# Queries and keys of a cross-attention projected with channels on the partitions, rotated between two banks, and carried to the score stacks by DMA through a scratch array

## The chip, the cores and the metric

The kernel runs on one core of a Trainium2 chip. The metric is the device time of one execution in microseconds. A run of the kernel is one launch that computes four chained layers; the change touches the first two of the kernel's phases, which belong to the first layer.

## The reference, cut to what matters

Four batches of 512 tokens with 256 channels. The first layer is an attention of 16 heads of 16 channels from the normalised tokens to a context of the same size:

```python
t = _layernorm(x)                                  # (4, 512, 256)
q = (t @ Wq.T + bq).reshape(B, L, 16, 16).transpose(0, 2, 1, 3)
k = (ctx @ Wk.T + bk).reshape(B, K, 16, 16).transpose(0, 2, 1, 3)
v = (ctx @ Wv.T + bv).reshape(B, K, 16, 16).transpose(0, 2, 1, 3)
# rotation: x * cos + rotate_half(x) * sin, rotate_half = concat([-x2, x1]) of the two 8-channel halves
q, k = _apply_rope(q, cos_q, sin_q), _apply_rope(k, cos_k, sin_k)
attn = softmax(where(mask, q @ k^T * 16 ** -0.5, -inf))
x = x + tanh(g_xattn[0]) * mask * ((attn @ v) @ Wp.T + bp)
```

Three more layers follow (a mixture of experts, a second attention, a quantised feed-forward layer). The change doesn't touch them.

## The kernel before, in words

**The stacks.** `phase_attend` computes scores with matmuls whose two operands are "stacks": for every pair of heads, 128 partitions, 64 for each head (`ROWS`), and 512 tokens on the free axis. The 64 rows of a head are: three times 16 channels, so that high and low parts of the two operands give a product of near float32 precision (queries: high, high, low; keys: high, low, high), then four rows for the row maxima, one row for the mask, and rows of zeros. There are 32 pairs in all (8 for each batch), in `q_stacks` and `k_stacks`.

**phase_prepare** fills the stacks, tile by tile: 16 tiles (`T`) of 128 tokens with tokens on the partitions. For each tile TensorE transposes the normalised tokens (line 423), multiplies context by the key and value weights (430) and tokens by the query weights (436); VectorE adds the biases (292 to 297) and writes the values to `va`; GpSimd multiplies by cosine and sine (393 to 397); VectorE adds the two (303); ScalarE rounds the high parts into `stack` (347, 348); VectorE subtracts for the low parts (308, 310) and copies the mask (312); TensorE transposes `stack` 16 times, pair by pair (415), and ScalarE copies the result out of PSUM into `q_stacks` and `k_stacks` (355). `schedule` runs these as a software pipeline: engines work on tiles n+1, n, n-1, n-2 and n-3 in one step. Context arrives by tile through a pair of buffers, loaded from SP's queue (253).

**phase_attend** runs 16 steps (`STEPS`, four heads of one batch each). TensorE first computes scores only to find row maxima (500, 14 units of two heads ahead of use, `LEAD`), VectorE reduces them (562), GpSimd splits the maxima in two parts (`split`, 579 to 583), TensorE transposes these (510), ScalarE copies them (629), and GpSimd lowers the query stack by them (`lower`, 589). Then TensorE computes the scores again (518), ScalarE takes exponentials (638), and TensorE multiplies by the values (527). GpSimd also copies the values of a step to a padded tile (`stage_values`, 594) and adds a bias to one tile of x (`bias`, 600 and 604). Its order in step s is: `stage_values(s)`, `split(s + 1)`, `lower(s + 1)`, `bias(s)`. TensorE's order is written out in `block.tensor`; `values(s, 0)` waits for `v_ready`, `maxima(s + 1)` at key tile 2 waits for `mt_ready`.

Each phase is a block that all engines leave together before the next begins.

## Time and profile before

| | |
|---|---|
| Time before, median of 3 runs | 794.51 us (793.86 to 795.33) |
| Time of the profiled execution | 795.87 us |
| Its span, first to last instruction | 794.0 us |
| TensorE busy over the span | 689.2 us (87%) |
| VectorE busy | 473.1 us (60%) |
| ScalarE busy | 358.8 us (45%) |
| GpSimd busy | 283.2 us (36%) |
| Mean granted TensorE clock | 0.933 of full speed |

The shares of busy time are means over phases with different limits; what counts for this change is read from the stretch from 0 to about 180 us. A matmul in float32 appears as two records, so "x4" in a TensorE row are two products; in the scores of the attention a product is one record. In what follows PE is TensorE, DVE VectorE, ACT ScalarE, POOL GpSimd, SP SyncE, and a q behind the name is the engine's queue of DMA issues.

### The profile page before, as it was taken

What the parts mean: (1) busy time and instruction counts of PE and PEld (TensorE: products, weight loads), DVE (VectorE), ACT (ScalarE), POOL (GpSimd) and SP (SyncE); (2) the same over time, 40 slices, a digit from 0 to 9 for tenths busy, and PEclk for the clock granted to TensorE, in tenths of its full rate; (3) what the DMA queues carried; (4) which work ended last, traced back from release to release, by engine and by line L of the source; (5) the groups of instructions that cost most, each with busy time, mean ns of one, the idle gap of its engine ahead of it and who ended that gap; (6) DMA issues with size and microseconds to landing.
All of it is one profiled execution on the core that took longest, in us unless ns stands there. A gap on an engine that the chain in (4) does not pass through costs nothing. (4 is left out here: it accounts for less than half of the span.)

```text
span 794.0 us, 10607 instructions
## 1 busy us (share of the span) xinstructions
PE 689.2 (87%) x3503; PEld 441.0 (56%) x3522; DVE 473.1 (60%) x852; ACT 358.8 (45%) x644; POOL 283.2 (36%) x462
## 2 busy tenths in 40 slices
PE   3599959999999996878999999995699999966986
PEld 1277733433344333745777777774376776852554
DVE  3567658888888841746834343434355546447985
ACT  0156644888888886345432222431313031102665
POOL 1446523344433450580001010101040436246897
PEclk9799986999999999989999999998789899986999
DMA  6000000000000004800100000001100000000001
GB/s 195 14 27 26 20 8 0 1 1 1 1 1 1 1 1 164 314 15 0 70 37 1 1 0 0 1 0 43 25 1 0 1 1 0 1 0 2 26 33 47
DMA packets 14103, 21.43 MB, mean 27 GB/s; under 512 B 2161, under 2 KB 11505, under 8 KB 13297
## 3 DMA queue, kind: packets, MB, share of 16 engines
q1 hardware_dynamic: 13200, 20.34, 7.5%
q10 hardware_dynamic: 864, 0.59, 0.3%
q8 instruction: 23, 0.38, 0.2%
q14 instruction: 16, 0.12, 0.1%
HBM read 18.83 MB, written 2.10 MB: 26 GB/s over the span
## 5 line engine op out<-in xcount | busy, mean ns | idle before, releaser
L562 DVE TENSOR_REDUCE mx<-ps_f 128x2 f32<-128x1024 f32 x128 | 151.5, 1220 | 31.6 <-PE ps_f L500 31.3
L638 ACT ACTIVATE prob<-ps_s 128x512 f32<-128x512 f32 x256 | 134.6, 608 | 34.5 <-PE ps_s L518 34.5
L518 PE MATMUL ps_s<-q_stacks,k_stacks 64*128 64x512 f32 x256 | 90.2, 484 | 5.9 <-ACT prob L638 3.5
L518 PEld LDWEIGHTS ps_s<-q_stacks,k_stacks 64*128 64x128 f32 x256 | 35.8, 188 | 87.2 <-ACT prob L638 70.9
L500 PE MATMUL ps_f<-k_stacks,q_stacks 64*128 64x512 f32 x256 | 63.8, 449 | 6.8 <-DVE mx L562 5.3
L527 PE MATMUL ps_o<-prob,vst 128*32 128x512 f32 x512 | 69.0, 612 | 0.0
L1018 ACT ACTIVATE qs<-ps_g 128x512 f32<-128x512 f32 x40 | 23.9, 598 | 88.6 <-PE ps_u L902 88.6
L1085 DVE SCALAR_TENSOR_TENSOR h<-ps_u,most,qs 128x512 f32<-128x512 f32 x32 | 24.0, 751 | 62.5 <-ACT qs L1018 62.5
L589 POOL TENSOR_TENSOR q_stacks<-minus,q_stacks 128x1024 fp32r<-128x1024 f32 x16 | 38.0, 2372 | 55.0 <-ACT minus L629 55.0
L172 POOL TENSOR_TENSOR norm_tmp_att<-st 128x4 f32<-128x4 f32 x4 | 1.0, 240 | 142.4 <-DVE st L1124 142.4
L1527 ACT ACTIVATE qs<-ps_SC,nmax 128x512 f32<-128x512 f32 x16 | 11.0, 686 | 76.4 <-DVE nmax L1415 76.4
L1091 DVE TENSOR_TENSOR h_low<-h,h_high 128x512 fp32r<-128x512 f32 x40 | 27.6, 691 | 23.4 <-ACT h_high L1022 23.2
L1022 ACT CAST h_high<-h 128x512 fp32r<-128x512 f32 x40 | 24.8, 621 | 31.2 <-DVE h L1085 31.2
L500 PEld LDWEIGHTS ps_f<-k_stacks,q_stacks 64*128 64x128 f32 x256 | 30.8, 197 | 14.2 <-DVE mx L562 11.7
L393 POOL TENSOR_TENSOR qkr<-qkb,c 128x512 f32<-128x512 f32 x16 | 20.3, 1268 | 42.5 <-DVE stack L312 30.1
L1299 PE MATMUL ps_SC<-ks 128*128 128x512 f32 x64 | 31.8, 644 | 3.3 <-DVE ks L1409 2.3
L347 ACT CAST stack<-qkr 128x512 fp32r<-128x512 f32 x16 | 9.9, 618 | 54.0 <-DVE qkr L303 30.8
L430 PE MATMUL ps_kv<-wkv,ctxT 128*128 128x512 f32 x64 | 34.3, 663 | 0.0
L415 PE MATMUL ps_st<-c,stack 128*128 128x128 f32 x256 | 30.8, 274 | 3.9 <-ACT q_stacks L355 3.9
L1317 PE MATMUL ps_q<-ks,qs 128*128 128x256 f32 x128 | 30.9, 384 | 1.5 <-DVE hq L1444 1.5
L415 PEld LDWEIGHTS ps_st<-c,stack 128*128 128x128 f32 x256 | 28.7, 142 | 6.3 <-DVE stack L312 2.3
L916 PE MATMUL ps_yE<-h_high,down_low 128*128 128x512 f32 x80 | 32.1, 402 | 0.0
(278 smaller groups left out, 1524.2 us busy)
## 6 DMA issues: line engine op xcount, KB each, us to landing
up<-in_up SPq DMA_DIRECT2D x10, 256.0 KB, 6.7
x<-in_x SPq DMA_DIRECT2D x4, 512.0 KB, 8.0
ctxT<-in_ctxT SPq DMA_DIRECT2D x16, 128.0 KB, 2.1
ks<-in_ctxTC SPq DMA_DIRECT2D x1, 2048.0 KB, 13.3
ks<-in_ctx SPq DMA_DIRECT2D x1, 2048.0 KB, 18.8
out<-x SPq DMA_DIRECT2D x16, 128.0 KB, 1.7
down<-in_down SPq DMA_DIRECT2D x1, 1280.0 KB, 5.5
ks<-in_wqv SPq DMA_DIRECT2D x1, 1024.0 KB, 20.7
```

What stands on the lines that cost most here:

```text
L415: last = pe.transpose(ps_st[i][:, p, :], stack[:, u, i // 2, 2 * pair:2 * pair + 2, :] .rearrange("p h r -> p (h r)"), id32)
L430: last = pe.matmul(ps_kv[u][:, :, :], ctxT[:, u, c, :], wkv[:, c, :, :], start=(c == 0), stop=(c == DC - 1))
L500: last = pe.matmul(ps_f[n % 2][:, h, :], qs[rows(h), 2 * f + pair, qt * P:(qt + 1) * P], ks[rows(h), 2 * f + pair, :], start=True, stop=True)
L518: pe.matmul(ps_s[n % 3][:, :], ks[rows(h), 2 * s + pair, kt * P:(kt + 1) * P], qs[rows(h), 2 * s + pair, :], start=True, stop=True).then_i ...
L527: last = pe.matmul(ps_o[HPAD * j:HPAD * (j + 1), :], vst[:, s % 2, kt, HPAD * j:HPAD * (j + 1)], prob[:, kt % 2, j, :], start=(kt == 0), s ...
L562: dve.tensor_reduce(mx[:, f % 2, qt, 2 * pair:2 * pair + 2], ps_f[n % 2][:, :, :], AX_X, ALU.max).then_inc(used, 1)
L589: pool.tensor_tensor(own, minus[:, :, :].broadcast_to([P, 2, S]), own.bitcast(F32), ALU.add)\
L638: act.activation(prob[:, kt % 2, j, :], ps_s[n % 3][:, :], ACT.Exp, scale=SCALE)\
L916: pe.matmul(ps_y[half][:, :], down_low[:, e, own], h_high[:, u, :], start=False, stop=False)
L1091: dve.tensor_tensor(h_low[:, u, :], h32[:, u, :], h_high[:, u, :].bitcast(F32), ALU.subtract)\
L1299: last = pe.matmul(ps_S[q % 2][:, :], sT[:, c, q * P:(q + 1) * P], ctxT[:, c, ds(b * S, S)], start=(c == 0), stop=(c == DC - 1))
L1317: last = pe.matmul(ps_q[:, :], attT[:, q % 2, k, :], ctok[:, ds(b * QT + k, 1), :], start=(k == 0), stop=(k == QT - 1))
```

## The change

**What it does.** Queries and keys are computed with channels on the partitions and a whole batch (512 tokens) on the free axis, in two banks of 128 channels (the columns of the weights are sorted on the host so that bank 0 holds the first halves of all heads, bank 1 the second halves). The rotation then is: bank times cosine, bank times sine, and a difference and a sum between the banks (`turn_parts` on VectorE, `add_parts` on GpSimd). High parts are rounded on ScalarE, low parts subtracted on VectorE for keys (`low_k`) and GpSimd for queries (`low_q`), in place over `part`. The 16 stack transposes per tile and the copies behind them are gone. Instead SP writes high and low parts, 512 KB each, to a scratch array in HBM (`Stacks.write`), and GpSimd reads them back into the rows of the stacks (`Stacks.read`: six DMAs for a batch's queries or keys, 16 partitions and 256 KB each). The fixed rows and the mask row also come by GpSimd's DMAs. Reads of batches 0 and 1 (keys) lie in `phase_prepare`, those of batch 1 (queries), 2 and 3 in `phase_attend`, in GpSimd's order ahead of `stage_values`. Normalising moves from VectorE to ScalarE. Context comes by batch, and the loads of batches 2 and 3 lie in SP's queue behind writes.

```diff
-C_ID, C_COS, C_SIN, C_TRI, C32 = 0, 128, 192, 256, 320
+C_ID, C_TRI, C32 = 0, 128, 192
...
+        turned["spent"] = [parts, summed, high_done, k_low, q_low, q_done, v_done, v_copied, k_done, xT_done]
         @block.sync
...
+            def load_ctx(b):
+                if b > 1:
+                    sp.wait_ge(k_done, b - 1)
+                    sp.wait_ge(v_done, QT * (b - 1))
+                sp.dma_start(ctx_raw[:, b % 2, :, :], a["ctxTC"][:, :, b * S:(b + 1) * S]).then_inc(ctx_in[b % 2], 16)
             load_x(0)
+            sp.dma_start(wk, a["wk"]).then_inc(wk_in, 16)
+            load_ctx(0)
+            sp.dma_start(trig[:, :, :], a["trig"]).then_inc(wk_in, 16)
+            sp.dma_start(wv[:, :, :], a["wv"]).then_inc(weights, 16)
+            sp.dma_start(wq[:, :, :], a["wq"]).then_inc(weights, 16)
+            load_x(1)
+            load_ctx(1)
+            for b in range(2, B):
                 load_x(b)
+            for b in range(B):
+                sp.wait_ge(high_done, 2 * b + 1)
+                stacks.write(sp, "k", b, 0, k_out)
+                sp.wait_ge(k_low, b + 1)
+                stacks.write(sp, "k", b, 1, k_out)
+                if b + 2 < B:
+                    load_ctx(b + 2)
+                sp.wait_ge(high_done, 2 * b + 2)
+                stacks.write(sp, "q", b, 0, turned["q_out"])
+                sp.wait_ge(q_low, b + 1)
+                stacks.write(sp, "q", b, 1, turned["q_out"])
+            sp.wait_ge(k_out, 32 * B)
+        @block.tensor
+        def _(pe):
+            def keys(b):
+                pe.wait_ge(ctx_in[b % 2], 16 * (b // 2 + 1))
+                wait(pe, parts, 2 * b - 1)
+                for c in range(DC):
+                    for d in range(DC):
+                        last = pe.matmul(ps_k[c][:, :], wk[:, d, c * P:(c + 1) * P], ctx_raw[:, b % 2, d, :],
+                                         start=(d == 0), stop=(d == DC - 1))
+                last.then_inc(k_done, 1)
+            def queries(b):
+                pe.wait_ge(xT_copied, b + 1)
+                wait(pe, parts, 2 * b)
+                for c in range(DC):
+                    for d in range(DC):
+                        last = pe.matmul(ps_q[c][:, :], wq[:, d, c * P:(c + 1) * P], xnT[:, d, :], start=(d == 0),
+                                         stop=(d == DC - 1))
+                last.then_inc(q_done, 1)
+            def values(b):
+                for q in range(QT):
+                    if q % 2 == 0:
+                        wait(pe, v_copied, QT * (b - 1) + q + 2)
+                    for d in range(DC):
+                        last = pe.matmul(ps_v[q // 2][:, q % 2, :], ctx_raw[:, b % 2, d, q * P:(q + 1) * P], wv[:, d, :],
+                                         start=(d == 0), stop=(d == DC - 1))
+                    last.then_inc(v_done, 1)
+            def transposes(b):
+                wait(pe, xT_copied, b)
+                for q in range(QT):
+                    pe.wait_ge(xn_ready, QT * b + q + 1)
+                    for c in range(DC):
+                        last = pe.transpose(ps_T[:, c, q * P:(q + 1) * P], xn[:, q, c * P:(c + 1) * P], id32)
+                last.then_inc(xT_done, 1)
+            pe.wait_ge(wk_in, 32)
+            keys(0)
...
+            for b in range(B):
+                if b:
+                    keys(b)
+                transposes(b)
+                values(b)
+                queries(b)
         @block.vector
         def _(dve):
+            def turn_parts(b, which):
+                done, held, out = ((k_done, ps_k, k_out), (q_done, ps_q, turned["q_out"]))[which]
+                n = 2 * b + which
+                dve.wait_ge(done, b + 1)
+                wait(dve, out, 32 * b)
+                wait(dve, summed, n)
+                for c in range(DC):
+                    dve.scalar_tensor_tensor(out=part[which][:, c, :], in0=held[c][:, :], scalar=bqk[:, which, c:c + 1],
+                                             in1=trig[:, 0, :], op0=ALU.add, op1=ALU.mult)
+                for c in range(DC):
+                    last = dve.scalar_tensor_tensor(out=turn[:, 1 - c, :], in0=held[c][:, :],
+                                                    scalar=bqk[:, which, c:c + 1], in1=trig[:, 1, :], op0=ALU.add,
+                                                    op1=ALU.mult)
+                last.then_inc(parts, 1)
+            def low_k(b):
+                dve.wait_ge(high_done, 2 * b + 1)
+                dve.tensor_tensor(low[OF_K][:, :, :], part[OF_K][:, :, :], high[OF_K][:, :, :].bitcast(F32), ALU.subtract)\
+                   .then_inc(k_low, 1)
...
+            for b in range(B):
...
+                turn_parts(b, OF_K)
...
+                    ln_vector(dve, b + 1, (QT * (b + 1), QT * (b + 2)))
+                copy_values(b)
+                low_k(b)
+                turn_parts(b, OF_Q)
         @block.scalar
         def _(act):
+            def normalise(b):
+                act.wait_ge(rstd_ready, b + 2)
+                wait(act, xT_done, b)
+                for q in range(QT):
+                    t = QT * b + q
+                    act.activation(xn[:, q, :], x_sb[:, t, :], ACT.Identity, bias=less_mean[:, t:t + 1])\
+                       .then_inc(centred, 1)
+                for q in range(QT):
+                    t = QT * b + q
+                    act.wait_ge(centred, t + 1)
+                    act.activation(xn[:, q, :], xn[:, q, :], ACT.Copy, scale=rstd[:, t:t + 1]).then_inc(xn_ready, 1)
+            def transposed(b):
+                act.wait_ge(xT_done, b + 1)
+                wait(act, q_done, b)
+                act.copy(xnT[:, :, :], ps_T[:, :, :]).then_inc(xT_copied, 1)
+            def high_part(b, which):
+                act.wait_ge(summed, 2 * b + which + 1)
+                act.copy(high[which][:, :, :], part[which][:, :, :]).then_inc(high_done, 1)
...
+            for b in range(B):
+                transposed(b)
+                high_part(b, OF_K)
+                if b + 1 < B:
+                    normalise(b + 1)
+                high_part(b, OF_Q)
         @block.gpsimd
         def _(pool):
+            def add_parts(b, which):
+                pool.wait_ge(parts, 2 * b + which + 1)
+                pool.tensor_tensor(part[which][:, 0, :], part[which][:, 0, :], turn[:, 0, :], ALU.subtract)
+                pool.tensor_tensor(part[which][:, 1, :], part[which][:, 1, :], turn[:, 1, :], ALU.add).then_inc(summed, 1)
+            def low_q(b):
+                pool.wait_ge(high_done, 2 * b + 2)
+                pool.tensor_tensor(low[OF_Q][:, :, :], part[OF_Q][:, :, :], high[OF_Q][:, :, :].bitcast(F32), ALU.subtract)\
+                    .then_inc(q_low, 1)
             ln_pool(pool, 0, (0, QT))
+            stacks.fixed_rows(pool, "q", 0, B - 1)
+            stacks.fixed_rows(pool, "k", 0, B - 1)
+            pool.wait_ge(mask_done, 2)
+            for b in range(B - 1):
+                stacks.mask_row(pool, b)
+            for b in range(B):
+                add_parts(b, OF_K)
+                if b:
+                    low_q(b - 1)
+                if b == 1:
+                    pool.wait_ge(k_out, 32)
+                    stacks.read(pool, "k", 0)
+                if b == 2:
+                    pool.wait_ge(turned["q_out"], 32)
+                    stacks.read(pool, "q", 0)
+                if b == 3:
+                    pool.wait_ge(k_out, 32 * 2)
+                    stacks.read(pool, "k", 1)
+                if b + 1 < B:
+                    ln_pool(pool, b + 1, (QT * (b + 1), QT * (b + 2)))
+                add_parts(b, OF_Q)
+            low_q(B - 1)
+class Stacks:
...
+    def fixed_rows(self, pool, name, b, batches):
+        for h in range(2):
+            at = ROWS * h + MAX_ROW
+            n = ROWS - MAX_ROW - (name == "k")
+            dst = self.to[name][at:at + n, 8 * b:8 * (b + batches), :].rearrange("r (s a) n -> r s (a n)", a=2)
+            pool.dma_start(dst, self.a[name + "rows"].broadcast_to([n, 4 * batches, 2 * S])).then_inc(self.landed[b], 16)
+    def mask_row(self, pool, b):
+        for h in range(2):
...
+            pool.dma_start(self.to["k"][at:at + 1, 8 * b:8 * b + 8, :], src).then_inc(self.landed[b], 16)
+    def write(self, sp, name, b, part, out):
+        src = self.turned["low" if part else "high"][name == "q"]
+        sp.dma_start(self.a["room_" + name][b, part], src[:, :, :].bitcast(F32)).then_inc(out, 16)
+    def read(self, pool, name, b):
+        for o, part in enumerate((0, 0, 1) if name == "q" else (0, 1, 0)):
+            src = self.a["room_" + name][b, part].rearrange("(s a i) c n -> a (i c) s n", a=2, s=H // 2)
+            for h in range(2):
+                at = ROWS * h + HD * o
+                pool.dma_start(self.to[name][at:at + HD, 8 * b:8 * b + 8, :], src[h]).then_inc(self.landed[b], 16)
 def phase_attend(...)
...
+                if n % (UNITS * NG) == 0:
+                    pe.wait_ge(turned["landed"][f // NG], 16 * (14 + 4 * (f in (0, STEPS - NG))))
...
+            def stacks_ahead(s):
+                if s == 0:
+                    pool.wait_ge(turned["q_out"], 32 * B)
+                if s == 1:
+                    stacks.read(pool, "k", 2)
+                if s == 2:
+                    stacks.read(pool, "q", 2)
+                if s == 4:
+                    stacks.fixed_rows(pool, "k", 3, 1)
+                    stacks.mask_row(pool, 3)
+                    stacks.read(pool, "k", 3)
+                if s == 5:
+                    stacks.fixed_rows(pool, "q", 3, 1)
+                    stacks.read(pool, "q", 3)
+            pool.wait_ge(turned["q_out"], 32 * 2)
+            stacks.read(pool, "q", 1)
...
             for s in range(STEPS):
+                stacks_ahead(s)
                 if s > 1:
                     stage_values(s, s % 2)
```

All lines of the former tile pipeline in `phase_prepare` are removed. `part` and `low` are one piece of memory, for keys and for queries.

## Rows read from the trace of the kernel before

**Rows 1.** Busy time by stretch: start and end, length, each engine's us (instructions), clock, DMA
```profile
30.00:40.00 10.00, 3.78 (x6) 1.83 (x7) 5.01 (x19) 1.14 (x2) 4.58 (x4) 0.58 0.04 14
60.00:70.00 10.00, 10.00 (x62) 7.79 (x61) 7.39 (x22) 6.67 (x14) 6.19 (x8) 1.00 0.09 26
...
120.00:130.00 10.00, 8.38 (x30) 4.36 (x28) 9.14 (x9) 4.00 (x8) 3.18 (x6) 0.50 0.00 0
...
150.00:160.00 10.00, 9.82 (x64) 4.12 (x66) 8.35 (x8) 8.34 (x17) 3.73 (x6) 1.00 0.00 0
```

**Rows 2.** Timeline at the seam of the two phases: start, duration, instruction
```profile
108.06 1.18 ACT L355 CAST k_stacks<-ps_st 128x512 fp32r<-128x512 f32 x2
109.49 0.34 SPq L490 DMA_DIRECT2D bp<-in_bp  x1
```

**Rows 3.** Timeline of PE in the preparation, 36 to 50 us
```profile
36.70 3.62 PE L430 MATMUL ps_kv<-wkv,ctxT 128*128 128x512 f32 x4
...
43.76 1.88 PE L430 MATMUL ps_kv<-wkv,ctxT 128*128 128x512 f32 x4
45.48 1.03 PE L436 MATMUL ps_qA<-wq,xnT 128*128 128x256 f32 x4
...
48.09 0.38 PE L423 MATMUL ps_T<-c,xn 128*128 128x128 f32 x2
48.31 1.88 PE L430 MATMUL ps_kv<-wkv,ctxT 128*128 128x512 f32 x4
```

**Rows 4.** Throughput of the DMA engines, 40 slices of 4 us from 0 to 160 us
```profile
GB/s 43 342 358 192 33 0 33 33 2 0 33 12 25 33 33 33 33 33 33 26 7 33 33 2 0 0 4 34 1 0 0 0 0 0 0 0 4 0 0 0
```

**Rows 5.** Groups of DVE and ACT instructions: count, busy us, mean ns, idle time before
```profile
L1085 DVE SCALAR_TENSOR_TENSOR h<-ps_u,most,qs 128x512 f32<-128x512 f32 x32 | 24.0, 751 | 62.5 <-ACT qs L1018 62.5
L1107 DVE TENSOR_TENSOR x_low<-qs,x_high 128x1024 fp32r<-128x1024 f32 x4 | 5.1, 1274 | 2.4 <-ACT x_high L1006 2.3
...
L1006 ACT CAST x_high<-qs 128x1024 fp32r<-128x1024 f32 x4 | 4.2, 1052 | 0.0
```

**Rows 6.** Groups of POOL instructions
```profile
L589 POOL TENSOR_TENSOR q_stacks<-minus,q_stacks 128x1024 fp32r<-128x1024 f32 x16 | 38.0, 2372 | 55.0 <-ACT minus L629 55.0
L393 POOL TENSOR_TENSOR qkr<-qkb,c 128x512 f32<-128x512 f32 x16 | 20.3, 1268 | 42.5 <-DVE stack L312 30.1 <-DVE qkb L297 12.4
...
L148 POOL TENSOR_TENSOR rstdA<-lntmpA,powerA 128x4 f32<-128x4 f32 x1 | 1.0, 1034 | 6.9 <-DVE lntmpA L139 6.9
```

**Rows 7.** DMA issues over the whole run: count, KB each, median us from issue to landing
```profile
x<-in_x SPq DMA_DIRECT2D x4, 512.0 KB, 8.0
...
out<-x SPq DMA_DIRECT2D x16, 128.0 KB, 1.7
```

**Rows 8.** Timeline of the issues of two DMAs over 128 partitions, on SP's and ACT's queue
```profile
1.25 0.66 SPq L249 DMA_DIRECT2D wkv<-in_wk  x1
...
3.33 1.03 ACTq L368 DMA_DIRECT2D bv<-in_bv  x1
```

**Rows 9.** Timeline of POOL: first split, one step, start of the next
```profile
119.43 0.29 POOL L579 TENSOR_SCALAR mt<-mx 128x16 fp32r<-128x16 f32 x1 [7.07 <-DVE mx L562]
...
159.66 0.61 POOL L600 TENSOR_TENSOR gated<-bp,coef 128x256 f32<-128x256 f32 x1
...
161.03 0.42 POOL L594 COPY vst<-va 128x272 f32<-128x272 f32 x1
164.15 0.27 POOL L579 TENSOR_SCALAR mt<-mx 128x16 fp32r<-128x16 f32 x1 [2.70 <-DVE mx L562]
...
164.82 0.27 POOL L583 TENSOR_SCALAR mt<-mt 128x16 f32<-128x16 f32 x1
...
170.88 0.60 POOL L600 TENSOR_TENSOR gated<-bp,coef 128x256 f32<-128x256 f32 x1
```

**Rows 10.** Timeline of PE in the same step
```profile
165.29 1.07 PE L527 MATMUL ps_o<-prob,vst 128*32 128x512 f32 x8
...
166.96 0.66 PE L510 MATMUL ps_s<-c,mt 128*128 128x128 f32 x4
```

304 lines of the change are left out of this document (97 added, 207 removed).

## The prediction

> **What bounds the kernel now.** I read the profile from the outside in. The table of stretches shows where the change lies: once it runs, PE is busy for all 10 us of a stretch of the preparation at full clock, with DVE at 7.4 and POOL at 6.2 [rows 1]; before that there is a slow start, with PE at 3.8 of 10 us and a clock of 0.58. The timeline at the seam says when the preparation ends: the last copy out of PSUM ends at 109.2 us and the attention's first DMA is issued at 109.5 [rows 2]. The timeline of PE gives the pitch: from one key and value product to the next it is 48.31 - 43.76 = 4.55 us for a tile [rows 3], so PE's work per tile, the 16 stack transposes among it, sets the pace. In the attention PE is busy for 9.8 of 10 us, DVE and ACT for 8.3 [rows 1]: whatever stalls PE there lengthens the kernel by the same amount, and POOL, with 3.7 us of 10, has room. Its step lasts 170.88 - 159.66 = 11.2 us [rows 9].
>
> **PE's share of the preparation.** Two float32 products with 512 columns take 1.88 us at full clock, 3.62 at the low one; two with 256 columns take 1.03, two transposes 0.38 [rows 3]. A batch now costs PE 4 products of 512 for keys and 4 for queries (3.8 us each), 8 of 256 for values (some 3.8) and 8 transposes (1.5): 12.9 us, against 4 x 4.55 = 18.2 before. So PE would need 52 us for four batches and no longer sets the pace, unless its clock stays low.
>
> **The start.** Before keys(0) the loads of x (512 KB), wk (256), context (512), trig (512) and about 100 KB of constants must land. The DMA engines moved 0.17, 1.37 and 1.43 MB in the first three slices of 4 us [rows 4]. 1.9 MB are through at 9.1 us, and with a us for the receipt keys(0) starts at 10.2. The first products run at the low clock, as the product at 36.70 us did [rows 3]: 4 x 1.81 = 7.2, to 17.4. Transposes, values and queries at full clock take 9.1 more, to 26.5. turn_parts is four DVE instructions of 0.75 us [rows 5], which overlap a little: 2.8. add_parts is two POOL instructions of half the size of the 2.37 us one: 2.4 [rows 6]. So the queries' sum of batch 0 ends at 31.7. The keys' side of batch 0 is earlier: turn_parts ends at 20.2, when POOL has issued its ten DMAs for fixed rows and masks (10 + 10 x 0.8 = 18, price below).
>
> **The loop from batch to batch.** Three loops are closed in the new code, and the longest one sets the pitch.
> The first runs through HBM: `low_q` lies in the memory of `part`, so turn_parts of the queries waits until the low part of the batch before is written (`q_out`), and POOL makes that low part only behind the keys' sum. In order: turn_parts K 2.8, add_parts 2.4, low_q 2.4 [rows 5, 6], the write W, turn_parts Q 2.8, add_parts 2.4, which is 12.8 + W. For W the nearest rows are a store of 128 KB with 1.7 us to landing and loads of 512 KB, issued among others, with 8.0 [rows 7]; these are the bounds. The write has 512 KB and lands beside POOL's six reads of 256 KB, so I take 5.0, between the two. Pitch: 17.8.
> The second runs through POOL: add_parts Q 2.4, wait for turn_parts K 2.8, add_parts K 2.4, low_q 2.4, six DMA issues at d each, the power 1.0 [rows 6]: 11.0 + 6d. It becomes the longest at d = 1.13.
> The third spans two batches: power, normalising on ACT (eight instructions of some 0.4, my estimate from 1.05 us for four times the elements [rows 5]: 3.2), values and queries 7.6, then turn and add of queries and keys 10.4, low_q 2.4, 6d, 1.0, some 25 + 6d for two batches, 15 for one at d = 0.8. ScalarE has some 7 us of work in a batch and DVE 12; neither binds.
> So three pitches of 17.8 from 31.7 lead to 85.1. Behind it stand the last high part 1.05 [rows 5], low_q 2.4 and an issue with the change of blocks 0.9: 89.4. PE now has 12.9 us of work in 17.8, with pauses of some us in front of the transposes, and the clock was at 0.58 with PE at 3.8 of 10 us in the old preparation and at 0.50 in the attention's first steps with PE at 8.4 of 10 [rows 1]. One batch's values and queries at the low clock would cost 7.6 more, all of them hidden where that loop has slack; I add 3. Preparation ends at 92.5 and gives 109.2 - 92.5 = 16.7 us.
>
> A page of the Trainium skill, "DMA: Bandwidth & Descriptors" (Anatomy of one DMA), gives about 2.0 us and bytes over 436 GB/s for a DMA, which is 3.2 us for such a write. By it the sum would be 3 x 1.8 = 5.4 us lower. The store of 128 KB above took 1.7, less than the page's 2.3, and the loads in a crowd took far more than its formula, so I stay with the rows.
>
> **What is given back in the attention.** POOL issues its DMAs ahead of `stage_values(s)`: 6 at s = 1 and 2, 10 at s = 4, 8 at s = 5. Behind them on POOL are the copy of the values, which PE needs for values(s, 0), and split(s + 1), which PE needs for the transposed maxima. The rows give the slack: the copy ended at 161.45 and the product that uses it began at 165.29: 3.84 us. The split waited 2.70 us for DVE, and was done at 165.09 where PE came to it at 166.96 [rows 9, 10]: 4.6, and 5.0 at s = 1, where there is no copy. Past the slack, PE stands still, and DVE and ACT behind it.
> The price d of one issue on POOL is not in the trace, since POOL issued no DMA. Bounds: 0.34 us, the shortest issue on SP [rows 2], and 1.9, if POOL stands to the 1.03 us of the dearest issue over 128 partitions [rows 8] as its elementwise work stands to DVE's (2.37 against 1.27 for 1,024 elements [rows 5, 6]). A read has 128 runs of 2 KB, as many as the two issues of [rows 8] have partitions; I take 0.8 between these. Then 6 issues cost 4.8: nothing at s = 1, 1.0 at s = 2; 8.0 - 3.84 = 4.2 at s = 4; 6.4 - 3.84 = 2.6 at s = 5. Sum 7.8. The six issues at the head of the attention are free: POOL waited 7.07 us for DVE before its first split [rows 9]. If that cover were gone they would cost 4.8.
> The waits of PE on the landing of a batch cost nothing in the forecast: batch 0's reads are issued by 63 us, batch 1's by 97 and needed in step 2, some 35 us on; later ones have longer.
> The same page says that a DMA from GpSimd is prepared in software with about 1 us to the first byte, against 0.6 us from SP or ACT. No row here shows it. With d = 1.0 the sum of the stalls would be 1.0 + 2.2 + 6.2 + 4.2 = 13.6.
>
> **Sum.** -16.7 + 7.8 = -8.9. Against the profiled execution, 795.87 - 8.9 = 787.0; that one lay 1.4 us over the median of 794.51, so I predict 786.
>
> **Rivals.**
> 1. *POOL's issues are dear, and the kernel gets slower.* The mechanism is the one place of PE's wait for the copied values and the split. At d = 1.1 stalls of 1.6 + 2.8 + 7.2 + 5.0 = 16.6 use up the gain: above 1.1 the kernel is slower. At d = 1.4 stalls are 3.4 + 4.6 + 10.2 + 7.4 = 25.6, POOL's loop is 19.4, which puts the seam at 97.3, and the sum is +13.7: 808. For it speaks that POOL is the slowest engine in each shared kind of work, against it the 0.66 us of an issue on SP [rows 8].
> 2. *POOL's issues are cheap and the write is quick.* d = 0.6 and W = 3: stalls 0 + 0 + 2.2 + 1.0 = 3.2, seam at 86.5, sum -19.5: 775. With d = 0.34, W = 1.7 and no cold batch the seam is at 79.6 and nothing is given back: 765.
> 3. *PE's clock stays low through the preparation.* Then 10.2 + 4 x 25.4 us and the tail of 9 give 121, and with the stalls +20: 814. For it speaks the clock of 0.50 to 0.58 with PE partly idle [rows 1], against it that keys, transposes and values run back to back for some 9 us in every batch.
> 4. *POOL's transfers are slow.* Fixed rows of 3.1 MB and batch 0's reads of 3.1 MB go through POOL's queue from 11 us on; below 6.3 MB / 81 us = 77 GB/s the first product of the attention waits. Each has a destination of 16 partitions; if rate followed partitions, an eighth of the 358 GB/s of [rows 4] would be 45 GB/s, the landing at 151, and the time near 844. The Trainium skill's "SBUF — State Buffer" (The DMA port swizzle) has it that the number of ports reached decides, and 16 neighbouring partitions reach 4 of 16; by that the rate would be some 109 GB/s and nothing would wait. No row here shows either.
> 5. *Gain and loss cancel*, d near 1.1, within 0.2%.
>
> **How the numbers follow.** Forecast (d 0.7 to 1.0, W 3.5 to 6.5) 0.36, its own range 778 to 793; rival 2 0.27; rival 5 0.07; rival 1 0.17; rival 4 0.07; rival 3 0.06. About 0.2% is what a measurement of this kernel tells from no change. Faster 0.36 + 0.27 = 0.63, same 0.07, slower 0.30. The range goes from 766, the low bounds of d and W, to 808, rival 1 at 1.4: outside are rival 4, most of rival 3 and the dear end of rival 1.
>
> **What the profile will show.** If I am right: the seam near 92; PE at 7 of 10 us in the preparation; DVE's turn_parts of the queries released by a DMA of q_out, or POOL's by d, with a pitch of 17 to 18; rows of POOL's queue near 0.8 us each; idle time of PE of 1, 4 and 3 us in steps 2, 4 and 5 and none in 1; from step 6 on the pitch of 11.2 as before, and nothing changed behind the attention. The prediction is wrong if POOL's issues cost over 1.1 us, if the write loop isn't the longest, if PE's first product waits for a landing, or if the clock in the preparation is at 0.5 throughout.

## The result, and the profile after

| | before | after |
|---|---|---|
| Median | 794.35 us (4 runs, 793.86 to 795.33) | 814.89 us (4 runs, 813.3 to 815.5) |
| Profiled execution, span | 795.87, 794.0 us | 815.22, 812.7 us |
| Seam | 109.5 us | 124.1 us |
| Seam to the end | 684.5 us | 688.6 us |

The ratio is 1.026 (95% interval 1.024 to 1.027): slower by 20 us, where 786 was forecast. The seam is the point at which the attention's first DMA is issued; "seam to the end" is the span less that point.

The busy times by stretch, against [rows 1]: between 40 and 50 us no compute engine does anything, yet the DMA engines move 225 GB/s.

```profile
30.00:40.00 10.00, 5.37 (x16) 2.57 (x14) 0.00 (x0) 1.96 (x2) 0.30 (x1) 0.92 1.31 136
40.00:50.00 10.00, 0.00 (x0) 0.00 (x0) 0.00 (x0) 0.00 (x0) 0.00 (x0) 0.50 1.03 225
60.00:70.00 10.00, 5.82 (x20) 5.05 (x21) 3.60 (x5) 5.26 (x10) 4.39 (x5) 0.66 1.42 187
...
126.00:138.00 12.00, 8.62 (x24) 3.52 (x24) 11.13 (x11) 0.59 (x1) 5.70 (x13) 0.50 1.40 120
```

DVE's timeline says what ends that silence. These are the first rows of turn_parts of the keys of batches 1, 2 and 3 and of the last low part; the bracket holds the idle time and who ended it:

```profile
50.09 1.41 DVE L328 SCALAR_TENSOR_TENSOR k_part<-ps_k,bqk,trig 128x512 f32<-128x512 f32 x2 [22.36 <-DMA room_k<-k_low_part]
...
59.66 1.21 DVE L338 TENSOR_TENSOR k_low_part<-k_part,k_high 128x1024 fp32r<-128x1024 f32 x1
...
74.34 1.41 DVE L328 SCALAR_TENSOR_TENSOR k_part<-ps_k,bqk,trig 128x512 f32<-128x512 f32 x2 [10.28 <-DMA room_k<-k_low_part]
...
98.21 1.41 DVE L328 SCALAR_TENSOR_TENSOR k_part<-ps_k,bqk,trig 128x512 f32<-128x512 f32 x2 [9.92 <-DMA room_k<-k_low_part]
```

The pitch is 23.9 to 24.3 us, and the sum by group (count, busy us, mean ns, idle time before) puts nearly all the waits on the keys' write, hardly any on the queries'. The last row is the price d of an issue on POOL:

```profile
L328 DVE SCALAR_TENSOR_TENSOR k_part<-ps_k,bqk,trig 128x512 f32<-128x512 f32 x8 | 5.6, 747 | 50.0 <-DMA room_k<-k_low_part 42.6 <-PE ps_k L278 7.5
L328 DVE SCALAR_TENSOR_TENSOR q_part<-ps_qA,bqk,trig 128x512 f32<-128x512 f32 x8 | 5.6, 745 | 3.4 <-DMA room_q<-q_low_part 2.5 <-issue 0.9
...
L477 POOL DMA_DIRECT2D k_stacks<-room_k x12 | 6.4, 537 | 0.0
```

The DMA issues up to 125 us (count, KB each, median us from issue to landing), against [rows 7], and below them the issues of 24 to 52 us, where the low part of batch 0's keys takes 24.9 us:

```profile
k_stacks<-room_k POOLq DMA_DIRECT2D x12, 256.0 KB, 11.0
...
room_k<-k_low_part SPq DMA_DIRECT2D x4, 512.0 KB, 13.2
...
room_q<-q_low_part SPq DMA_DIRECT2D x4, 512.0 KB, 3.5
q_stacks<-in_qrows POOLq DMA_DIRECT2D x2, 768.0 KB, 18.1
...
k_stacks<-in_krows POOLq DMA_DIRECT2D x2, 720.0 KB, 31.0
...
room_k<-k_low_part SPq DMA_DIRECT2D x1, 512.0 KB, 24.9
```

At the seam, against [rows 2], POOL has been idle for 5.92 us:

```profile
124.10 0.33 SPq L518 DMA_DIRECT2D bp<-in_bp  x1
124.11 0.95 POOL L599 MEMSET mt<- 128x1024 f32 x1 [5.92 <-POOLq L202]
```

The keys' last write is not what it waits for. POOL's reads of batch 1's keys, issued from 105.75 us on, landed up to 122.66, while that write had landed at 117.93. In the twelve runs in which DMAs of POOL's were still in flight when its last instruction ended, the seam followed 0.9 to 1.7 us behind the last landing; in e4, which has none, it followed POOL's last instruction by 0.8. So the blocks seem to change only when POOL's own DMAs have landed; no run tests that apart.

In the attention, against [rows 9], these are the starts of steps 4, 5 and 6 and what POOL issues in step 4:

```profile
185.46 0.61 POOL L632 TENSOR_TENSOR gated<-bp,coef 128x256 f32<-128x256 f32 x1
186.82 1.23 POOL L460 DMA_DIRECT2D k_stacks<-in_krows  x2
188.03 1.07 POOL L466 DMA_DIRECT2D k_stacks<-mrow  x2
189.10 3.15 POOL L477 DMA_DIRECT2D k_stacks<-room_k  x6
...
198.35 0.61 POOL L632 TENSOR_TENSOR gated<-bp,coef 128x256 f32<-128x256 f32 x1
...
210.03 0.61 POOL L632 TENSOR_TENSOR gated<-bp,coef 128x256 f32<-128x256 f32 x1
```

Step 4 lasts 12.89 instead of 11.2 us, step 5 11.68: stalls of 1.7 and 0.5.

### The profile page after: what moved, and what is told of

Read it like the earlier page. It is cut to its first block and busy times, and to the rows that moved or that the text cites. A ratio compares the mean times of both kernels' runs of the same rounds, so it can differ in the third digit from the quotient of the medians.

```text
span 812.7 us, 9603 instructions
## 1 busy us (share of the span) xinstructions
PE 665.6 (82%) x3266; PEld 415.4 (51%) x3266; DVE 462.2 (57%) x775; ACT 334.9 (41%) x592; POOL 304.2 (37%) x496
## 5 line engine op out<-in xcount | busy, mean ns | idle before, releaser
L1068 ACT ACTIVATE qs<-ps_g 128x512 f32<-128x512 f32 x40 | 23.9, 599 | 89.3 <-PE ps_u L952 89.2
L278 PE MATMUL ps_k<-ctx_raw,wk 128*128 128x512 f32 x32 | 19.4, 764 | 30.2 <-DVE turn L331 19.6
L1141 DVE TENSOR_TENSOR h_low<-h,h_high 128x512 fp32r<-128x512 f32 x40 | 27.6, 691 | 23.4 <-ACT h_high L1072 23.2
L328 DVE SCALAR_TENSOR_TENSOR k_part<-ps_k,bqk,trig 128x512 f32<-128x512 f32 x8 | 5.6, 747 | 50.0 <-DMA room_k<-k_low_part 42.6
L1611 POOL TENSOR_TENSOR ehT<-ks,hqT 128x256 f32<-128x256 f32 x16 | 11.8, 741 | 55.5 <-DVE hqT L1498 40.9
L278 PEld LDWEIGHTS ps_k<-ctx_raw,wk 128*128 128x128 f32 x32 | 7.7, 251 | 40.8 <-issue 26.7
L1758 ACT ACTIVATE qs<-ps_gD,amax 128x1024 f32<-128x1024 f32 x16 | 17.8, 1115 | 25.5 <-PE ps_gD L1796 25.5
## 6 DMA issues: line engine op xcount, KB each, us to landing
k_stacks<-room_k POOLq DMA_DIRECT2D x24, 256.0 KB, 10.3
ctx_raw<-in_ctxTC SPq DMA_DIRECT2D x4, 512.0 KB, 16.7
```

Of the source, the lines that this page charges most:

```text
L278: last = pe.matmul(ps_k[c][:, :], wk[:, d, c * P:(c + 1) * P], ctx_raw[:, b % 2, d, :], start=(d == 0), stop=(d == DC - 1))
L1141: dve.tensor_tensor(h_low[:, u, :], h32[:, u, :], h_high[:, u, :].bitcast(F32), ALU.subtract)\
```

## The experiments

Theory 1: the DMAs with destinations of 16 partitions on POOL's queue hold up SP's writes, and DVE waits for the write of the keys' low part because `low` lies in the memory of `part`. The rival, theory 2: a write of 512 KB to HBM is slow by itself. Letters behind a theory's number are local to the run that they stand with. In e1, e3 and e4 a block of zeros ahead moves the first load from 0.74 to 18.20 us, so 17.5 us are to be taken off every point of time and off the total.

**e3_no_fixed: no fixed rows of batches 0 to 2.**

```diff
-            stacks.fixed_rows(pool, "q", 0, B - 1)
-            stacks.fixed_rows(pool, "k", 0, B - 1)
```

> Leaves out the four DMAs of fixed rows of batches 0 to 2 (3 MB), with both stacks set to zero in a block of some 17 us ahead of everything, so times count from the first load. Theory 1 (the writes to the scratch array stand behind GpSimd's transfers on the shared DMA engines): the wait of 22.4 us in front of the keys' turn_parts of batch 1 falls to under 6, the later two waits of 10 us stay, and the seam of the phases comes some 17 us earlier, near 107 us from the start of the loads. Theory 2 (a write of 512 KB to HBM is slow by itself, 10 us or more): the first wait falls to about 10 at most and the seam by under 13.

813.25 us, or 795.8 without the zeros; seam 124.4 - 17.5 = 106.9. The wait of 22.4 us is gone, the two of 10 us are there. Without the 3 MB of constants the first wait doesn't come about.

**e4_no_early: no DMA of POOL's for batches 0 to 2.**

```diff
-            stacks.fixed_rows(...)       # "q" and "k", batches 0 to 2, and their mask rows
-                    stacks.read(...)     # all reads of batches 0 to 2
```

> Leaves out every GpSimd DMA of batches 0 to 2 (fixed rows, masks, reads), with the same block of zeros ahead; the scores of these batches are zero. The writes to the scratch array stay. Theory 1: each write of 512 KB lands within 3 to 4 us, no turn_parts waits over 2 us for it, the pitch of a batch is near 15 us and the seam near 85 us from the start of the loads (39 earlier than in the changed kernel). Theory 2: writes still land after 10 us, the pitch stays near 24.

789.01 us, or 771.5 without the zeros; seam 100.2 - 17.5 = 82.7. SP's writes are unchanged, but land in 2.6 to 3.5 us (medians; 3 to 4 were expected), and turn_parts of the keys is released by POOL's sum, at a pitch of 16.1:

```profile
64.17 1.41 DVE L328 SCALAR_TENSOR_TENSOR k_part<-ps_k,bqk,trig 128x512 f32<-128x512 f32 x2 [2.70 <-POOL q_part L419]
80.28 1.41 DVE L328 SCALAR_TENSOR_TENSOR k_part<-ps_k,bqk,trig 128x512 f32<-128x512 f32 x2 [2.70 <-POOL q_part L419]
```

```profile
room_k<-k_low_part SPq DMA_DIRECT2D x4, 512.0 KB, 2.9
room_q<-q_high SPq DMA_DIRECT2D x4, 512.0 KB, 2.6
```

**e1_spread: batch 0 to 2's reads to 128 partitions, same bytes.**

```diff
-                pool.dma_start(self.to[name][at:at + HD, 8 * b:8 * b + 8, :], src[h])...
+                pool.dma_start(self.to[name][:, at, :], self.a["zeros"][:, h, :])...   # at = 8 * b + 2 * o + h
```

> The six reads of each set (batches 0 to 2) have the same bytes, run length and number of runs, but each goes to one slot of all 128 partitions in place of eight slots of 16 partitions; they read an array of zeros in HBM. Fixed rows stay narrow. Block of zeros ahead. Theory 1a (the narrow destination makes GpSimd's transfers slow): a set of 1.6 MB lands in 5 us in place of 13, the waits of 10 us in front of batches 2 and 3 fall under 5, that of batch 1 (22 us) stays, the seam comes some 12 us earlier. Theory 1b (the software queue or the rounding on the way makes them slow): the rate stays near 120 GB/s and the waits as they were.

820.43 us; seam 129.3 - 17.5 = 111.8, 12.3 us earlier than with narrow reads. The first wait stays at 22.45, the others fall to 5.9 and 6.4 us, where under 5 was expected.

**e5_probe: narrow and wide transfers by themselves**, ahead of the changed kernel.

```diff
+ for o in range(3): for h in range(2):
+   eng.dma_start(to[64 * h + 16 * o:64 * h + 16 * o + 16, :, :], rows16[h])   # narrow
+   eng.dma_start(to[:, 2 * o + h, :], rows128[h])                             # wide
```

> A block ahead of the changed kernel moves seven sets of six DMAs of 256 KB from HBM, one set after the other, each awaited: GpSimd to 16 partitions with rounding, GpSimd to 16 without, GpSimd to 128 partitions with rounding, to 128 without, SP to 16, SP to 128, and SP with ACT to 16 each at once. Theory 1a: sets to 16 partitions take some 13 us whatever the queue, sets to 128 some 5. Theory 1b: GpSimd's sets take 13 us whatever the width, SP's 5; if rounding is the cost, only the sets with it.

The last column is GB/s. In order: POOL narrow with rounding, POOL narrow, POOL wide with rounding, POOL wide, SP narrow, SP wide, SP and ACT narrow at once, each into its own half:

```profile
2.00:14.00 12.00, 0.00 (x0) 0.00 (x0) 0.00 (x0) 0.00 (x0) 2.74 (x6) 1.00 1.43 130
18.00:29.00 11.00, 0.00 (x0) 0.00 (x0) 0.00 (x0) 0.00 (x0) 1.36 (x3) 1.00 1.03 133
31.00:37.00 6.00, 0.00 (x0) 0.00 (x0) 0.00 (x0) 0.00 (x0) 3.14 (x6) 1.00 0.81 229
39.00:44.00 5.00, 0.00 (x0) 0.00 (x0) 0.00 (x0) 0.00 (x0) 2.73 (x6) 1.00 0.76 250
47.00:58.00 11.00, 0.00 (x0) 0.00 (x0) 0.00 (x0) 0.00 (x0) 0.00 (x0) 1.00 1.00 139
60.00:66.00 6.00, 0.00 (x0) 0.00 (x0) 0.00 (x0) 0.00 (x0) 0.00 (x0) 1.00 0.82 260
68.00:79.00 11.00, 0.00 (x0) 0.00 (x0) 0.00 (x0) 0.00 (x0) 0.00 (x0) 1.00 1.02 141
```

Neither the queue nor the rounding matters much; the destination does. From first issue to last landing a narrow set took 13.3 to 14.6 us, a wide one 7.1 to 7.9, not the 5 expected. Two queues, each into its own half of the partitions, move no more together than one queue that alternates between the halves.

**e9_width: how wide is wide enough, and what it does to a write.** The same six DMAs of 256 KB from SP on 16, 32, 64 and 128 neighbouring partitions and on 16 that lie eight apart; then a write beside a crowd on ACT's queue.

> Edit: a block of transfers ahead of the changed kernel, some 75 us of it, the rest as it is. From SP's queue five sets of six DMAs, 256 KB each in 128 runs of 2 KB: 16 neighbouring partitions, 32, 64, 128, and 16 partitions eight apart. Then from ACT's queue six of the narrow ones, with one write of 512 KB from SP's queue behind the first of them; the same with six of the wide ones; and the write alone. Theory A (the rate follows the ports of the SBUF that the partitions reach: 4, 8, 8, 16 and 8 of 16): 13, 7, 7, 5 and 7 us. Theory B (the rate follows the number of partitions, whichever they are): 13, 7, 4 to 5, 4 to 5 and 13 us. For the write both have: over 8 us behind narrow reads, 4 to 6 behind wide ones, 3 alone; the rival, that a write is only slow by its share of the bytes, has the same time in both crowds.

Rates in that order (last column); the sixth row is the narrow crowd with the write in it, and below stands the landing of the write in the narrow crowd, in the wide crowd and alone:

```profile
5.00:14.00 9.00, 0.00 (x0) 0.00 (x0) 0.00 (x0) 0.00 (x0) 0.00 (x0) 1.00 1.08 121
20.00:26.00 6.00, 0.00 (x0) 0.00 (x0) 0.00 (x0) 0.00 (x0) 0.00 (x0) 1.00 1.03 214
29.00:35.00 6.00, 0.00 (x0) 0.00 (x0) 0.00 (x0) 0.00 (x0) 0.00 (x0) 1.00 1.02 230
38.00:41.00 3.00, 0.00 (x0) 0.00 (x0) 0.00 (x0) 0.00 (x0) 0.00 (x0) 1.00 0.98 308
44.00:50.00 6.00, 0.00 (x0) 0.00 (x0) 0.00 (x0) 0.00 (x0) 0.00 (x0) 1.00 0.98 215
56.00:65.00 9.00, 0.00 (x0) 0.00 (x0) 0.00 (x0) 0.00 (x0) 0.00 (x0) 1.00 1.08 120
...
room_q<-q_high SPq DMA_DIRECT2D x1, 512.0 KB, 11.5
...
room_q<-q_high SPq DMA_DIRECT2D x1, 512.0 KB, 6.5
...
room_q<-q_high SPq DMA_DIRECT2D x1, 512.0 KB, 2.6
```

For these transfers theory A's order holds: 64 partitions are hardly better than 32 (230 against 214), and 16 partitions spread out are as good as 32 neighbours (215); the five times were 15.6, 9.4, 9.1, 6.8 and 9.7 us, a fifth to two fifths above those expected. By the port formula of the Trainium skill's "SBUF — State Buffer" (Door 1: The DMA port swizzle) these reach 8 of 16 ports, 16 neighbours reach 4. Its asymptotes are 109 and 218 GB/s; measured are 121 (130 to 141 in e5) and 214 to 230, so the ratio agrees and the narrow rate lies above the page's. The same page says that two DMAs into the two halves at once serialize; e5's last row, 141 GB/s, agrees.

The write in the narrow crowd was issued at 57.55 us and landed at 69.09. It didn't share the engines: from 58 to 65.5 us ACT's queue moved 490 packets and SP's none, and from 65.5 to 69.2 SP's 144 and ACT's last 59.

**e13_small_packets and e14_half_reads: how the queues share the engines.** e13 sends each fixed-row DMA as two, with runs of 2 KB instead of 4; e14 sends three of the six reads of batch 0's keys later.

```diff
-            pool.dma_start(dst, self.a[name + "rows"].broadcast_to([n, 4 * batches, 2 * S]))...
+            for a in range(2):
+                dst = self.to[name][at:at + n, 8 * b + a:8 * (b + batches):2, :]
+                pool.dma_start(dst, self.a[name + "rows"][:, :, a * S:(a + 1) * S].broadcast_to(...))...
```
```diff
-                    stacks.read(pool, "k", 0)
+                    stacks.read(pool, "k", 0, (0,))                       # b == 1
...
-                    stacks.read(pool, "k", 1)
+                    stacks.read(pool, "k", 0, (1,)); stacks.read(pool, "k", 1, (0,))   # b == 3; the rest at the head of the attention
```

> Edit: the changed kernel with the fixed rows of a half sent in two DMAs of 2 KB packets instead of one of 4 KB packets; the same rows, partitions and bytes. Nothing is left out. Theory 1a (the two queues take turns packet by packet, and the narrow packets set the pace of both): against 4 KB packets a queue of 2 KB packets gets a third of some 125 GB/s, against 2 KB packets half of it; the write of the keys' low part of batch 0 lands after 14 to 19 us instead of 25, the first wait in front of turn_parts of the keys shrinks from 22.4 to 11 to 17 us, the other two stay at 10; four more issues on GpSimd at the start and two in steps 4 and 5 cost 1 to 3 us; time 806 to 812 us. Theory 1b (the write waits until all narrow bytes that were sent before it are through): the bytes are the same, the wait stays at 21 to 24 us and the time at 815 to 818 us.

> Edit: the changed kernel with only three of the six reads of batch 0's keys (one half of the stacks) where all six stood; the other three go where batch 1's keys were read, three of whose six go to the head of the attention. Nothing is left out. Theory 1a (turns packet by packet): the 512 packets of SP's queue (keys' high and low part of batch 1) now have turns with 384 narrow packets instead of 512 of 768; the second wait shrinks from 10.3 to 6 to 9 us, and that the doubled reads added nothing there is the other end of the same curve; the first wait (22 us) and the third (10) stay. Time 809 to 814 us. Theory 1b (all narrow bytes sent before it): 3 reads are 6 us less, the second wait is 4 to 5 us. Rival (the wait doesn't depend on the reads): it stays at 10 us.

The second row of turn_parts of the keys in e13, and the third in e14:

```profile
42.33 1.41 DVE L328 SCALAR_TENSOR_TENSOR k_part<-ps_k,bqk,trig 128x512 f32<-128x512 f32 x2 [15.21 <-DMA room_k<-k_low_part]
```

```profile
69.37 1.41 DVE L328 SCALAR_TENSOR_TENSOR k_part<-ps_k,bqk,trig 128x512 f32<-128x512 f32 x2 [5.72 <-DMA room_k<-k_low_part]
```

With the same bytes in smaller runs the first wait fell from 22.4 to 15.2 us (the write landed after 17.7 instead of 24.9; 809.05 us in all), though the last fixed rows landed no sooner, at 46.4 us instead of 44.7. That is the queues taking turns, not a write behind all bytes sent before it. The packet counts of the two queues show the turns directly. From 16 to 32 us of the changed kernel POOL's queue moved 441 packets with 1.62 MB and SP's 441 with 0.45 MB; in e13 it was 830 and 765. SP's packets have 1 KB on average, and they are not the write's: they are the rows of x of batches 2 and 3 (1 MB), which SP had issued before it. The second of these loads, issued at 7.11 us, landed at 48.17; the keys' low part, behind it in the same queue, at 50.01. So 1 MB in small packets ahead of the first write took turns with POOL's packets of 4 KB. At this stretch's 27.6 packets per us the 256 packets of the keys' high and low part, issued from 22.9 us on, would have taken 9 us by themselves: an estimate of 32 to 35 us for the landing instead of 50. No run moved these loads, so that is not tested.

In e14 the second wait fell from 10.3 to 5.7, below the 6 to 9 of the turns and above the 4 to 5 of the other theory: the wait depends on the reads, but the run doesn't choose between the two. (Its count of packets was off as well: a write goes in 128 packets of 4 KB, so high and low part are those 256, not 512.) The third wait stayed at 10.1; 808.92 us.

**e11_twice and e10_wide_reads.** e11 sends batch 0's key reads twice; e10 writes the high part twice to the scratch array so that a read is one DMA over 48 partitions.

```diff
+                    stacks.read(pool, "k", 0, 1)      # e11: again, into batch 1's rows
...
+        all_three = self.a["room_" + name][b].rearrange("(s a i) u c n -> a (i u c) s n", a=2, s=H // 2)   # e10
+            to = self.to[name][ROWS * h:ROWS * h + MAX_ROW, 8 * b:8 * b + 8, :]
+            pool.dma_start(to, all_three[h])...
```

> Edit: the changed kernel with the suspected cost doubled in one place. The six reads of batch 0's keys are sent a second time right behind the first, into the rows of batch 1, which get their own later. Theory 1: the write of the low part of the keys of batch 1 now stands behind 3.1 MB at some 125 GB/s instead of 1.6; the wait in front of turn_parts of the keys of batch 2 grows from 10 us by 10 to 13, the first wait (22 us) stays, and the time grows by as much, to 824 to 829 us. Rival (the write waits for something else, its own length or the engines' order): the waits stay as they are, the time grows by 0 to 3 us, which the six more issues on GpSimd may cost.

> Edit: the changed kernel with wide reads. The high part is written twice to the scratch array, beside the low part, so that the 48 rows of a half of the stacks are one DMA over 48 neighbouring partitions, 768 KB (rows in another order, the same for queries and keys, which leaves the sums of products the same). Two reads for a batch's queries or keys instead of six, the same bytes; the write of the high part has 1 MB instead of 0.5. Fixed rows as they are. Theory 1 (the width of the destination sets the rate, and the reads hold up the write of the keys' low part): a batch's reads take 7 to 8 us instead of 13, the second and third wait in front of turn_parts of the keys shrink from 10 to 3 to 6 us each, the first of 22 us, which is the fixed rows', stays; with two issues instead of six on GpSimd the stalls in steps 4 and 5 are gone. Seam at 109 to 116, time 796 to 805 us. Rival (bytes or the number of transfers in flight count, not the width): the waits stay at 10 us or grow with the larger write, time 812 us or more.

Both expectations failed. In e11 (814.42 us) the second wait stayed at 9.93. Seen afterwards, the write had landed at 73.1 us and the sixth of POOL's reads landed only at 76.4, so the six added behind them came too late to matter. The extra reads delayed something else, turn_parts of the queries of batch 2 (7.5 us idle), and the third key wait shrank to 2.7, so nothing was added. In e10 (807.34 us) the waits are 23.2, 8.8 and 8.2. A high part of 1 MB now stands ahead of the low part in SP's queue, so the run weighs two changes against each other and doesn't isolate the width. Nor were its reads quick: over 48 partitions they moved 132 GB/s from 124 to 136 us, where almost nothing else went, against 120 for the narrow ones, and the queries of batch 1 took 14.1 us instead of 15.2, not 7 to 8. That doesn't fit theory A, which gives 48 neighbours the rate of 32. Why they are slow here, and not in e9, is open.

**e6_late_fixed and e7_two_k: the two remedies apart.** e6 sends batch 1's and 2's fixed rows at the head of the attention; e7 keeps the order and gives the keys' high and low parts two copies.

```diff
-            stacks.fixed_rows(pool, "q", 0, B - 1)
+            stacks.fixed_rows(pool, "q", 0, 1)            # e6; "k" likewise
...
-                wait(dve, out, 32 * b)
+                wait(dve, out[b % 2], 32 * (b // 2))      # e7, keys only; part, high, low indexed by b % 2
```

> Edit: ahead of the preparation only batch 0's fixed rows are sent (1 MB); those of batches 1 and 2 (2 MB) go behind the reads at the head of the attention. Nothing is left out of the computation. Theory 1 (the fixed rows, 16 partitions wide, hold the DMA engines when the low part of the keys of batch 0 is to be written): 1 MB at about 130 GB/s is through at 20 us, the write is issued at 25 us and lands in under 8 us; the wait of 22.4 us in front of turn_parts of the keys of batch 1 goes, the two waits of 10 us behind it stay, the seam comes at 107 to 108 and the time is 796 to 800 us. Rival (the write is late because of the crowd of loads at the start, or the reads that follow): that wait stays above 10 us and the time above 804 us.

> Edit: two copies of the keys' high part and low part, used in turn (the second lies in the rows of batch 3, which are filled much later); DMAs and their order are as in the changed kernel. Nothing is left out. Theory 1 (slow writes, and someone who waits for them): the writes of the keys' low parts land as late as now, 25 and 13 us, but VectorE's turn_parts of the keys no longer waits for them; the wait moves to GpSimd in front of batch 0's reads (k_out) and to turn_parts of the queries (q_out). So part of the 42.6 us of waits comes back as others: seam 106 to 118, time 795 to 809 us. Rival (the memory shared by parts is the whole cause, the slow transfers are not): the pitch falls to 15 to 16 us at once, seam 84 to 88, time 773 to 778 us. Second rival (the wait is only a symptom of another chain): seam 122 to 126.

e6: 797.94 us, seam 105.8 (107 to 108 expected); the first wait gone, the others 10.3 and 9.9. e7: 793.0 us, 2 us below the range, seam 102.7 (106 to 118). As expected POOL now waits for the write, though only once. What was not expected: DVE waits for the same queue all the same, 16 us, for x of batches 2 and 3. Afterwards turn_parts of the keys goes at 16.7:

```profile
48.52 1.41 DVE L121 BATCH_NORM_STATS2 st<-x 128x6 f32<-128x256 f32 x4 [16.04 <-DMA x<-in_x]
...
50.70 3.19 POOL L482 DMA_DIRECT2D k_stacks<-room_k  x6 [13.36 <-DMA room_k<-k_low_part]
```

**e8_all and e12_all_wide: both remedies, and transfers spread over the steps.** Two copies for queries too; fixed rows batch by batch; no more than six issues in one step of the attention.

```diff
-                    pool.wait_ge(k_out, 32 * 2)
-                    stacks.read(pool, "k", 1)
+                    stacks.fixed_rows(pool, "q", 1, 1)
+                    stacks.fixed_rows(pool, "k", 1, 1)
...
+                if s in (1, 4):    # fixed rows of batches 2 and 3, and 3's mask row
+                if s in (2, 5):    # k reads;  s in (3, 6): q reads;  batch 1's: k at the head, q in step 0
```

> Edit: the candidate for a faster kernel. Two copies of high and low parts of keys and of queries; ahead of the preparation only batch 0's fixed rows, batch 1's where the keys of batch 1 were read; the reads of batch 1's keys at the head of the attention, its queries in step 0, then one group of at most six reads in each of steps 2, 3, 5 and 6, fixed rows in 1 and 4. Nothing is left out. Theory 1: no wait on a write is left, the pitch is set by GpSimd or by the chain through both engines, 14 to 16 us; batch 0's reads (24 us at 130 GB/s) end before the seam at 82 to 88; no stall in steps 4 and 5; time 766 to 776 us. Rival (the transfers cost as much wherever they stand, and the first product of batch 1 or batch 0 waits for its rows instead): time above 785 us.

> Edit: the faster candidate (two copies, spread transfers) with the wide reads. Theory 1: in the candidate no wait on a transfer was left, and the pitch of 16.1 us is VectorE's own work and one addition on GpSimd, which wide reads don't touch; only the tail and the first steps of the attention can gain. Seam at 83 to 86, time 768 to 772 us, the same as the candidate (771.7) within 0.4%. Rival (transfers still cost something in the candidate by slowing other loads and writes): below 767 us.

e8: 771.73 us (4 runs), ratio to before 0.970 (0.968 to 0.971). e12: 773.90 us (4 runs), 0.973 (0.971 to 0.975), 2 us above its range: reads over 48 partitions gain nothing. No write is waited for any more, as expected, but by e10 these reads are hardly quicker either, so the run doesn't show that quick transfers would be worth nothing. The seam is at 85.8 in e8. Its DVE has no gap from turn_parts of one batch's keys to the end of its queries', and then one wait for POOL:

```profile
31.46 1.41 DVE L333 SCALAR_TENSOR_TENSOR k_part<-ps_k,bqk,trig 128x512 f32<-128x512 f32 x2 [2.67 <-POOL q_part L424]
...
36.77 2.33 DVE L127 TENSOR_TENSOR lntmpA<-st 128x4 f32<-128x4 f32 x1
...
41.05 1.21 DVE L343 TENSOR_TENSOR k_low_part<-k_part,k_high 128x1024 fp32r<-128x1024 f32 x1
42.18 1.40 DVE L333 SCALAR_TENSOR_TENSOR q_part<-ps_qA,bqk,trig 128x512 f32<-128x512 f32 x2
43.50 1.40 DVE L336 SCALAR_TENSOR_TENSOR turn<-ps_qA,bqk,trig 128x512 f32<-128x512 f32 x2
47.61 1.41 DVE L333 SCALAR_TENSOR_TENSOR k_part<-ps_k,bqk,trig 128x512 f32<-128x512 f32 x2 [2.71 <-POOL q_part L424]
```

Every step of e8's attention lasts 11.2 us, but for the short last one.

## Why the prediction was wrong

**The step that failed** is "lands beside POOL's six reads of 256 KB, so I take 5.0": the write W, and with it the range of 1.7 to 8.0. The write that counts took 24.9 us for batch 0 and some 13 for batches 1 and 2, five and 2.6 times the forecast, because it had to share the engines with POOL's transfers, or wait for them, while these moved some 125 GB/s. Without them it takes 2.9 (e4). Beside it stood a second slip: the 3.1 MB of fixed rows were counted as issues on POOL and as a rival for the first product, never as traffic ahead of the first write, and the 1 MB of x that stands before that write in SP's own queue was not counted at all. Without the early fixed rows the seam comes 17 to 18 us sooner (e3, e6). In the forecast's own terms: from the queries' sum of batch 0 to that of batch 3 it took 84.4 us instead of 3 x 17.8 = 53.4, and all else up to the seam together 0.6 more than forecast.

**Which loop.** The forecast had the queries' write as the longest loop, 12.8 + W. The keys have a loop too, which was missing: from turn_parts over normalising sums and values to the end of `low_k` on DVE, 59.66 + 1.21 - 50.09 = 10.8 us, then the write, 13.1 to 13.5 with SP's step before it, which gives the 23.9 to 24.3 seen. With one W for both the queries' loop would be the longer; but the queries' low part is issued together with POOL's first read and lands in 3.5 us, the keys' goes out 3 us later, behind the high part, into the crowd.

**The floor.** With no write waited for the pitch is 16.1 (e4, e8). "Neither binds" was wrong for DVE: its work of a batch (13.4 us) and one wait of 2.7 for POOL's sum stand in series. The seam without any early transfer of POOL's, 82.7, is 10 us better than the forecast of 92.5, so the idea behind the gain was right and undersized: it was the transfers that turned -27 us at the seam into +15.

**The tail.** From POOL's last work to the seam the forecast has 0.9 us. It was 5.9, beside POOL's reads in flight. That the sum came out nearly right behind the loop is luck: the 3 us put in for the clock made up for part of it.

**The start** was right: keys(0) at 10.5 against 10.2, queries' sum at 30.3 against 31.7.

**d** is 0.53 us against 0.8, so stalls were 0, 0, 1.7, 0.5 instead of 0, 1.0, 4.2, 2.6. Rival 1 is refuted: the kernel got slower, but not by POOL's issues. Rival 2's cheap issues came true without its quick write.

**Rival 4** had the rate right and the victim wrong. With almost nothing beside them six reads ran at 120 GB/s [the row of 126 to 138 us above]; the Trainium skill's 109 GB/s ("SBUF — State Buffer", Door 1: The DMA port swizzle), named in the prediction, was the better estimate than 45. From it the prediction took "nothing would wait" for the first product, which held, and didn't ask about writes.

**The clock** fell to 0.50 in the idle stretch and PE's next products, the keys of batch 2, ran at the low level (6.56 us for what took 3.60 at 23.74), as in rival 3, but as a consequence: in e8 it is at 1.00 from 60 to 70 us. PE was busy for 56 of the 124 us, so it didn't set the pace; that rival 3's 814 us is the time measured is luck.

**The sum.** Forecast -16.7 + 7.8; measured +14.6 at the seam and +4.1 behind it. Of these the steps of the attention hold 1.9, seen in the 16 rows (first and last start) of either kernel:

```profile
L600 POOL TENSOR_TENSOR gated<-bp,coef x16: 602/612/630, 137.3 to 295.9; 128x256 f32<-128x256 f32 x16
```

```profile
L632 POOL TENSOR_TENSOR gated<-bp,coef x16: 608/611/622, 151.9 to 312.4; 128x256 f32<-128x256 f32 x16
```

From the last of them to the end it is 498.1 us before and 500.3 after, in phases that the change doesn't touch; in the profiles of all fifteen kernels here, these two among them, this part lay between 496.1 and 500.3, so these 2.2 us of the 20 are not explained by anything here.

**Left open.** That the traffic of POOL's queue makes the writes late is shown. How it does so is shown for the first wait alone: turns, packet by packet, with the loads of x ahead of the write. The second and third wait are not turns only. The keys' write of batch 1 was issued at 60.91 us, and from 64 to 68 us POOL's queue moved 267 packets and SP's 2. In e9 the write stood still for 8 us in the same way. What holds a write back before its first packet, and lets it go, no run shows.

## What to carry to other kernels

Before a transfer is moved to a queue "in the background", add up the time that it holds the DMA engines, at a rate measured for its own shape, and look for what else must cross them in that time and who waits for it: here constants that nobody needed before 124 us stopped DVE for 22, and for 10 of these every compute engine. Look at the writer's own queue too: loads in small packets ahead of a write delay it more than their bytes would say. A wait on a write is best removed at both ends, by a second copy of the buffer and by sending later what isn't needed yet; each alone gave 17 to 22 us, and both together, with the transfers spread, 43. When more of a suspected cost shows no effect, look at the idle times one by one before giving up the theory: the added part may have come too late, or the wait may have moved.

## What was not expected of the hardware

A DMA into 16 neighbouring partitions makes transfers on other queues slow too: 512 KB to HBM took 11.5 us beside six narrow reads, 6.5 beside six wide ones, 2.6 alone. The Trainium skill's "DMA: Bandwidth & Descriptors" (Queues, rings and completion order) says that an engine goes round the queues packet by packet; the changed kernel agrees from 16 to 32 us, with 441 packets of either queue, and e13, by the fall from 24.9 to 17.7 us when the other queue's runs were halved. The write in e9 doesn't show it: it was issued, and for 8 us the other queue alone moved packets. An issue of a read on GpSimd cost 0.53 us, between the 0.32 to 0.35 of SP's writes and the 0.66 of the SP load in [rows 8].
